# Attention layer and linear recurrence on one core: the recurrence laid out with key channels on partitions, in groups of 3, 3, 3, 3, 2, 2 batches instead of 4, 4, 4, 4

## Chip, cores and metric

One core of a Trainium2 chip runs the whole program. The metric is its device time in microseconds (us), lower is better. All data is float32.

## What is computed

The input has 16 batches of 112 rows of 512 channels and, per batch, a context of 375 rows. Two layers follow each other. The first is cross-attention with 16 heads of 32 channels and an MLP of inner width 2048. The second mixes each token with the one before it, runs a recurrence over time per head (32 heads of 16 key channels i and 16 value channels j), normalises its output per head, gates it, and ends with a squared-ReLU feed-forward part. Of the context, rows 0 and 1 and the rows 2 to 17 serve the second layer as the tokens before the first and as the start state.

```
attn = softmax(q @ k.T / sqrt(32) + mask) @ v            # layer 1, then c_proj, residual
y    = gelu(layernorm(h) @ fc_w + fc_b) @ proj_w         # MLP, residual
xm_j = xa + sx * (maa_stack_j + xxx_j)     j = 0..4      # token mixes: k, w, v, r, g
w    = exp(-exp(time_decay + tanh(xw @ td_w1) @ td_w2))
r, k, v, g = xr @ Wr.T, xk @ Wk.T, xv @ Wv.T, silu(xg @ Wg.T)
def step(s, (r, k, v, w)):                               # per head: s is 16 x 16, over 112 tokens
    a   = k[:, None] * v[None, :]
    out = sum_i r_i * (u_i * a_ij + s_ij)
    s   = a + w[:, None] * s
og   = groupnorm(out) * gn_w + gn_b;   x1 = x + (og * g) @ Wo.T
x1 + sigmoid(xr2 @ Wfr.T) * (relu(xk2 @ Wfk.T)**2 @ Wfv.T)
```

## The kernel before

The order is written out by hand, engine by engine, with semaphores. Batches go in groups of GB = 4, so the width of a group in tokens is T = 448. Products with a group's width hold 128 channels on the output's partitions and 448 tokens as columns.

The program of PE goes through groups g = 0 to 4. For g < 4 it does the *attention* of group g (`step`, 4 steps per batch, 16 in all), then the *MLP* of g (`mlp`). For g > 0 it does *post* of group p = g - 1 (Wo, layer norm, feed-forward, `post`), and for g < 4 the *token mix* of g (`pre`: low-rank products, decays, and the products for k, v, r and the gate). The recurrence of group p runs on DVE beside the attention and the MLP of g = p + 1. For the last group nothing is left to run beside it.

An attention step on PE is: the scores of the next step (`scores`, L304: four products onto one strip of rows each), the weighing of the values of the last step (`weigh`, L324: products onto 32 output partitions), and between four rounds of transposes (`turn`, L312, each waiting for ACT's exponents) the key and value projections of the next batch (L270). DVE takes the scores from PSUM, adds the mask and takes the row maximum (`masked`, L1020); ACT does the exponent and moves the transposed probabilities.

The recurrence (`scan_unit`) has one partition per batch and head (4 x 32 = 128). k, r and the decays w leave the token mix with channels on partitions, so POOL stores them to `rkw_scratch` and v to `v_scratch` in DRAM, and they are read back in the other layout. For each key channel i of 16, DVE makes r*u*k (L1067), k times v over all 16 value channels (L1069, 1792 columns with the start state at token 0, L1072), the sum of the bonus (L1075), two scans over time of 896 columns each (L1079, with the decays that ACT repeats for 8 value channels, L843), the product with r (L1083), and adds it to the output (L1091). These are UNITS = 5 sub-steps, UNITS_A_STEP = 3 of which stand in each attention step; the rest follows beside the MLP. In the last group the sum over i is done on PE with an identity product instead (`sum_channels`, L527). `group_norm` (L1100 to L1128) works in this layout; then SP writes `y_scratch` and reads it back with channels on partitions for `gate` (L1149, L1152).

The weights of the second half stream through a ring of SLOTS = 2 pieces of 1 MB each (`piece`, SP), 16 pieces per full group; a piece is loaded when the one two before it is used up. SP's queue is strict: the load of the start states, the wait for `y_norm` and the trip of y stand between ring pieces.

Of the kernel before, what the change touches and what calls it, by code (L numbers as in the profile page):

```python
# [5 lines left out]
F32 = mybir.dt.float32  # L6
# [11 lines left out]
GB = 4  # L18
NG = B // GB
# [4 lines left out]
JH = 8  # L24
# [13 lines left out]
ORDER = [1, 0, 2, 3, 4]  # L38

STORED = {1: 1, 2: 3, 3: 0}  # L40

W_MLP, W_POST, W_PRE = list(range(0, 8)), list(range(12, 16)), list(range(8, 12))


UNITS = 5
UNITS_A_STEP = 3
IN_STEPS = GB * HQ * UNITS_A_STEP

BLOCK = 2


def pieces_of(g):
    return [*(W_MLP if g < NG else []), *(W_POST if g > 0 else []), *(W_PRE if g < NG else [])]


PIECES = [p for g in range(NG + 1) for p in pieces_of(g)]
PIECE0 = [sum(len(pieces_of(k)) for k in range(g)) for g in range(NG + 1)]


# [30 lines left out]
def build(nc, x, ctxT, ctx, mask, shiftcols, cols, wq, wk, wv, wc, cproj_b, proj_b, stream,  # L90
          maa_w1, maa_w2, td_w1, td_w2, u, out):

    rkw_d = nc.dram_tensor("rkw_scratch", (B * RH, RS, 3, LQ), F32, kind="Internal").ap()
    v_d = nc.dram_tensor("v_scratch", (B * RH, RS * LQ), F32, kind="Internal").ap()
    y_d = nc.dram_tensor("y_scratch", (B * RH, RS * LQ), F32, kind="Internal").ap()

    ctxm = ExitStack()
    with ctxm:
# [6 lines left out]
        ident = sb("ident", [P, P])  # L105
        colt = sb("colt", [P, NCOL])
# [10 lines left out]
        ucol = sb("ucol", [P, RS])  # L117
# [14 lines left out]
        rden = sb("rden", [LQ, H])  # L132
        onT = sb("onT", [P, E, LQ])
# [9 lines left out]
        SX = sb("SX", [P, E * GB, LQ])  # L143
# [3 lines left out]

        VB = sb("VB", [P, RS, LQ])
        YB = sb("YB", [P, RS, LQ])
        rkw = sb("rkw", [P, 2, BLOCK, 3, LQ])  # L150
        s0 = sb("s0", [P, RS, RS])
        bon = sb("bon", [P, 2, LQ])
        gst = sb("gst", [P, 3, LQ])


        YT = SX[:, :, :].rearrange("p (e b) t -> p e (b t)", e=E)
        xnT = C[0]
        x_t = [HT[0:LQ, :, :].rearrange("p e t -> p (e t)")[:, k * D:(k + 1) * D] for k in range(2)]
        rdx = HT[0:LQ, :, :].rearrange("p e t -> p (e t)")[:, 2 * D:3 * D]
# [4 lines left out]
        XAs = XA[:, :, :, 1:LQ + 1]  # L164
        XAc = XA[:, :, :, :].rearrange("p e b t -> p (e b) t")
        wrep = XA[:, :, :, :].rearrange("p e b t -> p (e b t)")[:, 0:2 * JH * LQ].rearrange(
# [14 lines left out]
        def colb(name, n):  # L181
            k = COLS.index(name) * E
            return colt[:, k:k + E].unsqueeze(2).to_broadcast([P, E, n])
# [1164 lines left out]
```

## Time and profile before

| | us |
|---|---|
| median of 3 runs | 2032.33 |
| lowest and highest | 2018.66, 2036.81 |
| the profiled execution | 2021.98 |
| its span, first to last instruction | 2020.2 |
| PE busy in it | 1784.4 (88%) |
| DVE busy | 1176.1 (58%) |
| ACT busy | 637.1 (32%) |
| POOL busy | 223.3 (11%) |
| mean granted clock of TensorE | 0.92 |

An fp32 product appears as two matmul records; durations of neighbours overlap, so the pace is read from start to start. The granted clock has two levels, 1.00 (2.4 GHz) and 0.50 (1.2 GHz), and a mean says how much of a stretch ran at each. Idle PE is the length of a stretch less PE's busy time. "C<-..." names the tile written and the tiles read.

### The profile page before, as it was taken

To read this page: it belongs to the slowest core of one execution; us is meant where nothing else is said; L and a number is where in the kernel's file an instruction comes from. 1 tells how busy PE (TensorE), PEld (TensorE's weight loads), DVE (VectorE), ACT (ScalarE), POOL (GpSimd) and SP (SyncE) were. 2 spreads that over 40 slices of the span, in tenths; PEclk is the share of its full clock that TensorE was granted. 3 is DMA by queue.
4 is the path that set the end of the run, shared out by engine and by line. 5 is a ranking of instruction groups with operands and counts; after the bars stand their busy time and mean duration, and the time that the engine had idled before them with its cause. 6 is when DMAs were issued, how large, how long until landed. Compare 5 with 4: busy or idle time off the path is not lost.

```text
span 2020.2 us, 18127 instructions
## 1 busy us (share of the span) xinstructions
PE 1784.4 (88%) x6760; PEld 883.8 (44%) x6760; DVE 1176.1 (58%) x1649; ACT 637.1 (32%) x1480; POOL 223.3 (11%) x317
## 2 busy tenths in 40 slices
PE   6999998999999979999999979989779889856447
PEld 3555443445554433455554433445434334422223
DVE  1233002339988853449988654279988633299951
ACT  2566211136652112246641131256621131101011
POOL 1010000122210010122110010221200101100000
PEclk9999998799999989899999988999979987967868
DMA  7000021151102122341102321430012312400011
GB/s 234 26 26 21 22 83 63 62 160 33 40 27 77 63 99 81 96 125 40 53 14 71 105 76 60 128 97 32 14 34 84 103 47 85 146 25 21 7 57 39
DMA packets 73608, 135.15 MB, mean 67 GB/s; under 512 B 16241, under 2 KB 26993, under 8 KB 73521
## 3 DMA queue, kind: packets, MB, share of 16 engines
q1 hardware_dynamic: 59808, 101.05, 15.6%
q0 software_dynamic: 10496, 29.34, 4.7%
q10 hardware_dynamic: 3216, 3.60, 0.6%
q8 instruction: 55, 0.90, 0.2%
q14 instruction: 33, 0.26, 0.0%
HBM read 111.95 MB, written 22.02 MB: 66 GB/s over the span
## 4 chain that ended last, share of the span: by engine, by line
PE 68%; DVE 19%; issue 5%; DMA 3%; ACT 2%; ACTq 1%; POOL 1%; SPq 0%; DVEq 0%; POOLq 0%
PE bank L270 48%; PE bank L433 10%; DVE C L1079 5%; PE bank L497 3%; DVE sm L1020 3%; DVE C L1069 2%; PE bank L312 2%; DMA ring<-in_stream 2%; DVE YB L1091 1%; PE bank L304 1%; DVE C L1083 1%; DMA s<-in_ctx 1%; PE bank L324 1%; ACT XA L809 1%; PE bank L511 1%
## 5 line engine op out<-in xcount | busy, mean ns | idle before, releaser
L270 PE MATMUL bank<-C,ring 128*128 128x448 f32 x640 | 265.2, 577 | 17.9 <-DVE C L1131 17.9
L1079 DVE TENSOR_TENSOR_SCAN C<-XA,C 128x896 f32<-128x896 f32 x112 | 222.6, 2022 | 27.5 <-ACT XA L843 27.5
L433 PE MATMUL bank<-ring,HT 128*112 128x512 f32 x512 | 222.3, 592 | 0.0
L1020 DVE CUSTOM_DVE_ANT_0 sm<-bank,maskb 112x375 f32<-112x375 f32 x256 | 124.0, 541 | 166.5 <-PE bank L304 166.5
L270 PE MATMUL bank<-ctx_t,Wk 128*128 128x375 f32 x512 | 194.3, 504 | 13.4 <-DMA Wk<-in_wk 11.0
L270 PE MATMUL bank<-SX,ring 128*128 128x448 f32 x512 | 196.8, 543 | 7.8 <-ACT SX L809 7.8
L270 PEld LDWEIGHTS bank<-C,ring 128*128 128x128 f32 x640 | 128.5, 203 | 153.5 <-issue 149.6
L270 PE MATMUL bank<-Wv,ctx_t 128*125 128x512 f32 x384 | 182.3, 600 | 0.4 <-ACT C L809 0.4
L270 PE MATMUL bank<-ring,C 128*112 128x512 f32 x256 | 129.5, 662 | 56.1 <-issue 43.6
L312 PEld LDWEIGHTS bank<-ident,sm 112*125 112x125 f32 x768 | 123.5, 192 | 122.5 <-ACT sm L824 59.1
L830 ACT ACTIVATE probT<-bank 125x336 f32<-125x336 f32 x256 | 114.0, 445 | 145.8 <-PE bank L312 143.4
L824 ACT ACTIVATE sm<-sm,nm 112x375 f32<-112x375 f32 x256 | 153.5, 600 | 17.6 <-DVE nm L1020 17.3
L312 PE MATMUL bank<-ident,sm 112*125 112x112 f32 x768 | 128.3, 276 | 27.8 <-ACT probT L830 27.8
L433 PEld LDWEIGHTS bank<-ring,HT 128*112 128x112 f32 x512 | 90.6, 177 | 127.2 <-issue 127.2
L1232 DVE SCALAR_TENSOR_TENSOR C<-bank,colt,SX 128x448 f32<-128x448 f32 x80 | 53.6, 682 | 154.4 <-PE bank L497 152.7
L270 PEld LDWEIGHTS bank<-SX,ring 128*128 128x128 f32 x512 | 97.6, 191 | 104.6 <-issue 95.9
L891 ACT ACTIVATE HT<-bank,colt 128x448 f32<-128x448 f32 x64 | 40.5, 633 | 305.5 <-PE bank L270 305.5
L270 PEld LDWEIGHTS bank<-ctx_t,Wk 128*128 128x128 f32 x512 | 90.1, 195 | 62.0 <-issue 27.2
L1083 DVE TENSOR_TENSOR C<-C,rkw 128x1792 f32<-128x1792 f32 x56 | 113.3, 2023 | 1.8
L1069 DVE TENSOR_TENSOR C<-VB,rkw 128x1776 f32<-128x1776 f32 x56 | 112.0, 2001 | 0.1
L270 PEld LDWEIGHTS bank<-ring,C 128*112 128x112 f32 x256 | 49.8, 198 | 131.3 <-issue 119.9
L843 ACT ACTIVATE XA<-rkw 128x896 f32<-128x896 f32 x64 | 59.8, 949 | 131.4 <-DVE C L1083 68.1
(132 smaller groups left out, 2056.4 us busy)
## 6 DMA issues: line engine op xcount, KB each, us to landing
ring<-in_stream SPq DMA_DIRECT2D x64, 1024.0 KB, 5.5
ctx_t<-in_ctxT SPq DMA_DIRECT2D x16, 750.0 KB, 5.0
rkw_scratch<-HT POOLq DMA_DIRECT2D x48, 224.0 KB, 2.7
rkw<-rkw_scratch POOLq DMA_DIRECT2D x32, 224.0 KB, 3.1
HT<-in_x SPq DMA_DIRECT2D x16, 224.0 KB, 5.3
X<-in_x SPq DMA_DIRECT2D x16, 224.0 KB, 6.1
v_scratch<-HT POOLq DMA_DIRECT2D x16, 224.0 KB, 2.6
VB<-v_scratch SPq DMA_DIRECT2D x4, 896.0 KB, 7.1
```

The costliest lines, as they stand in the source:

```text
L270: last_ = nc.tensor.matmul(out_ap, pairs[k][0], pairs[k][1], start=(k == 0), stop=(k == len(pairs) - 1))
L312: last_ = nc.tensor.transpose(bank[k][0:KW, c * LQ:(c + 1) * LQ], sm[0:LQ, slot, c * KW:(c + 1) * KW], ident[0:LQ, 0:LQ])
L433: last_ = nc.tensor.matmul(bank[SC[b]][0:LQ, :], HT[:, c, b * LQ:(b + 1) * LQ], w[:, c, :], start=(m == 0 and c == 0), stop=(m == 3 and c ...
L497: closed(nc.tensor.matmul(bank[k][:, 0:T], w[:, e * P:(e + 1) * P], a, start=True, stop=True), ("LR", g, j, e), k)
L824: nc.scalar.activation(sm[0:LQ, slot, :], sm[0:LQ, slot, :], ACT.Exp, bias=nm[:, slot:slot + 1], scale=-1.0, accum_out=den[:, n % 2, e * H ...
L830: nc.scalar.activation(probT[:, r, :], tile(name)[0:KW, 0:KC * LQ], ACT.Copy).then_inc(freed(name), 1)
L843: nc.scalar.activation(wrep[:, i % 2, :].rearrange("p (j t) -> p j t", j=JH), rkw[:, (i // BLOCK) % 2, i % BLOCK, 2, :].unsqueeze(1).to_br ...
L1020: nc.vector.tensor_tensor_reduce(out=sm[0:LQ, slot, :], in0=tile(name)[0:LQ, 0:LK], in1=maskb[:, n % 2, :], scale=-SCALE, scalar=3.0e38, o ...
L1069: own.step(nc.vector.tensor_tensor(S[:, :, 1:LQ], VB[:, :, 0:LQ - 1], kk[:, 0:LQ - 1].unsqueeze(1).to_broadcast([P, RS, LQ - 1]), ALU.mult))
L1079: own.step(nc.vector.tensor_tensor_scan(out=part, data0=wrep[:, i % 2, :], data1=part, initial=0.0, op0=ALU.mult, op1=ALU.add))
L1083: prod = nc.vector.tensor_tensor(S[:, :, :], S[:, :, :], r.unsqueeze(1).to_broadcast([P, RS, LQ]), ALU.mult)
L1232: nc.vector.scalar_tensor_tensor(out=dst[:, e, :], in0=tile(name)[:, 0:T], scalar=col(f"maa_{ORDER[j]}", e), in1=SX[:, GB * e:GB * (e + 1) ...
```

## The change

Groups. The 16 batches go in six groups of 3, 3, 3, 3, 2 and 2, so widths are 336 and 224.

Layout. The recurrence now has the 128 key channels of eight heads on the partitions. k, r and the decays stay where the token mix leaves them (tiles KS, R and W). Only v goes through DRAM: POOL stores it, one token late, and reads it back per unit with each head's row repeated on its 16 key channels (`load_unit`). A unit is one of 4 channel blocks e and 4 value channels j of each head: 16 units a group, with columns j, batch, token (4 x 336 or 4 x 224). DVE does four sub-units on each (`sub_unit`): product with k, in place, and start state (L1221, L1224); a scan of half the columns (L1230), a scan of the other half; product with r (L1236). Three buffers take turns. There is no add on DVE: the sum over the key channels of a head is four products on PE per unit, each with a selecting matrix onto 32 output partitions (`sum_unit`, L418), for every group. DVE adds the finished block to the bonus (`y_add`, L1259). The decays are repeated by ACT once per block e instead of once per i, straight out of the exponent.

Bonus and norm. The bonus is r*u*k on DVE and one product per block with a matrix of heads (L632) in the token mix. Mean and variance per head are products with an averaging matrix (`means` L430, `variances` L437) between those of the MLP; ACT squares and takes Ln and Exp for the deviation; DVE applies norm and gate in four blocks. Nothing goes through DRAM and back.

Order. `Plan` holds at which attention step or at which of the 32 chunks of the MLP each sum stands, and how many of the 64 sub-units stand in the attention (44 of 12 steps for 3 after 3, 36 of 8 for 2 after 3, 48 of 8 for 2 after 2). Wo follows the MLP, or comes before its last quarter in the last group. The scores and exponents of the next group's first step now stand before the gate product. The token mix makes v first, then k, r and g. SP loads the start states after the ring's pieces as before, in group order, and has no trip of y. Weighed values share the bank of the transposes (6), and bank 7 collects the recurrence.

```diff
-GB = 4
-NG = B // GB
+SIZES = [3, 3, 3, 3, 2, 2]
...
-ORDER = [1, 0, 2, 3, 4]
+ORDER = [1, 2, 0, 3, 4]
...
+NJ = 4
+UNITS = E * (RS // NJ)
+STAGES = 4
+SUBS = UNITS * STAGES
+BUFS = 3
...
+IN_STEPS = {(3, 3): 44, (3, 2): 36, (2, 2): 48}
...
+            def sum_unit(p, unit):
+                e, q = divmod(unit, UNITS // E)
+                if q == 0:
+                    opened(Y_BANK)
+                pe.wait_ge(z_ready, p * UNITS + unit + 1)
+                n = width(p)
+                for s in range(NJ):
+                    last_ = nc.tensor.matmul(bank[Y_BANK][HD * s:HD * (s + 1), 0:n], sel[:, q, :],
+                                             unit_tile(p, unit)[:, s * n:(s + 1) * n],
+                                             start=(q == 0), stop=(q == UNITS // E - 1))
...
-            def sum_channels(p):
-                for k in SC:
-                    opened(k)
...
+            def load_unit(p, unit):
...
+                rows = v_d[p][e, q, :, :, :].rearrange("h s t -> h (s t)")
+                pool.dma_start(unit_tile(p, unit), rows.unsqueeze(1).to_broadcast([8, RS, NJ * width(p)])
+                               ).then_inc(s_in[unit % BUFS], 16)
...
-                elif stage == 4 and not last:
-                    own.settle()
-                    nc.vector.tensor_tensor(YB[:, :, :], YB[:, :, :], S[:, :, :], ALU.add).then_inc(scan_step, 1)
...
+                    own.step(nc.vector.tensor_tensor(
+                        S[:, :, :, 1:LQ], S[:, :, :, 1:LQ],
+                        KS[:, e, 0:n, 1:LQ].unsqueeze(1).to_broadcast([P, NJ, n, LQ - 1]), ALU.mult))
...
+                elif stage in (1, 2):
+                    own.settle()
+                    dve.wait_ge(wrep_ready, p * E + e + 1)
+                    part = flat[:, (stage - 1) * 2 * nt:stage * 2 * nt]
...
+                else:
+                    own.settle()
+                    js = flat.rearrange("p (j t) -> p j t", j=NJ)
+                    nc.vector.tensor_tensor(js, js, R[:, e, 0:nt].unsqueeze(1).to_broadcast([P, NJ, nt]), ALU.mult
+                                            ).then_inc(z_ready, 1)
```

DVE in the recurrence of the last group, before: one key channel for four batches.

```order
L1067 SCALAR_TENSOR_TENSOR bon<-rkw,ucol 128x112
L1069 TENSOR_TENSOR HT<-VB,rkw 128x16x111
L1072 COPY HT<-s 128x16
L1075 TENSOR_TENSOR bon<-bon 128x112
L1079 SCALAR_TENSOR_TENSOR HT<-XA,HT 128x896 x2
L1083 TENSOR_TENSOR HT<-HT,rkw 128x1792
```

The same place now: two units for two batches (the scans are printed as SCALAR_TENSOR_TENSOR in both).

```order
L1221 TENSOR_TENSOR C<-C,KS 128x8x111
L1224 COPY C<-s 128x8
L1230 SCALAR_TENSOR_TENSOR C<-XA,C 128x448 x2
L1236 TENSOR_TENSOR C<-C,R 128x896
L1221 TENSOR_TENSOR SA<-SA,KS 128x8x111
L1224 COPY SA<-s 128x8
L1230 SCALAR_TENSOR_TENSOR SA<-XA,SA 128x448 x2
L1236 TENSOR_TENSOR SA<-SA,R 128x896
```

The two small operations for the bonus have left; every remaining one is half as wide.

PE in the MLP of a group, before: products and nothing between them, then (not printed) the wait for Wo.

```order
L270 MATMUL bank<-SX,ring 128x448 x16
L433 MATMUL bank<-ring,HT 112x512 x16
L270 MATMUL bank<-SX,ring 128x448 x16
L433 MATMUL bank<-ring,HT 112x512 x16
L270 MATMUL bank<-SX,ring 128x448 x16
```

PE now, at the end of the MLP of group 4 (two batches, with the recurrence of three beside it).

```order
L418 MATMUL bank<-C,sel 32x336 x4
L334 MATMUL bank<-SX,ring 128x224 x12
L550 MATMUL bank<-ring,HT 112x512 x2
L418 MATMUL bank<-SA,sel 32x336 x4
L550 MATMUL bank<-ring,HT 112x512 x4
L430 MATMUL bank<-BV,mean 128x336 x4
L550 MATMUL bank<-ring,HT 112x512 x2
L437 MATMUL bank<-R,mean 128x336 x4
L334 MATMUL bank<-ring,C 112x512 x12
```

Two sums, the means and the variances (L418, L430, L437) have come between the MLP's products; the variances are its last and Wo (L334, ring,C) follows at once.

PE in an attention step now, with one sum (L418) between the second and third round of transposes, where there was none.

```order
L376 MATMUL bank<-ident,sm 125x112 x3
L418 MATMUL bank<-C,sel 32x336 x4
L334 MATMUL bank<-Wv,ctx_t 125x512 x2
L376 MATMUL bank<-ident,sm 125x112 x3
L334 MATMUL bank<-Wv,ctx_t 125x512 x2
```

The sum waits for DVE's product with r, and the transposes behind it wait with it.

## Rows read from the trace of the kernel before

**Rows 1.** Windows: length, busy PE, PEld, DVE, ACT, POOL, TensorE clock, DMA share, GB/s.
```profile
58.00:1762.00 1704.00, 1594.21 (x6378) 799.90 (x6376) 991.92 (x1468) 594.40 (x1406) 202.10 (x269) 0.94 0.21 67
58.00:209.00 151.00, 147.84 (x998) 86.84 (x996) 46.46 (x163) 90.88 (x252) 11.12 (x20) 1.00 0.08 25
331.00:437.00 106.00, 95.47 (x217) 43.83 (x216) 36.16 (x63) 22.18 (x44) 18.40 (x28) 0.79 0.26 81
437.00:595.00 158.00, 149.80 (x998) 86.64 (x996) 149.74 (x241) 101.22 (x263) 32.05 (x30) 1.00 0.18 55
722.00:795.00 73.00, 62.42 (x161) 28.00 (x162) 32.10 (x61) 18.64 (x45) 8.54 (x19) 0.91 0.13 43
1323.00:1478.00 155.00, 134.82 (x918) 80.05 (x917) 143.71 (x224) 91.06 (x239) 24.63 (x21) 0.92 0.12 39
1762.00:1912.00 150.00, 85.57 (x128) 35.69 (x128) 138.97 (x117) 16.64 (x18) 8.64 (x12) 0.72 0.09 28
1912.00:1940.00 28.00, 0.08 (x1) 0.11 (x1) 17.78 (x14) 0.39 (x1) 0.00 (x0) 0.59 0.20 66
```

**Rows 2.** Timeline of PE in an attention step of the second group.
```profile
459.48 0.90 PE L304 MATMUL bank<-KT,qT 32*112 32x375 f32 x8
460.31 0.78 PE L324 MATMUL bank<-probT,V 125*32 125x112 f32 x24
461.02 1.53 PE L270 MATMUL bank<-ctx_t,Wk 128*128 128x375 f32 x4
```

**Rows 3.** Timeline of PE from the MLP of the second group to its post.
```profile
665.43 12.19 PE L270 MATMUL bank<-SX,ring 128*128 128x448 f32 x32
677.46 13.90 PE L433 MATMUL bank<-ring,HT 128*112 128x512 f32 x32
691.19 12.19 PE L270 MATMUL bank<-SX,ring 128*128 128x448 f32 x32
...
722.42 15.54 PE L270 MATMUL bank<-ring,C 128*112 128x512 f32 x32 [5.31 <-issue]
...
740.93 1.06 PE L292 MATMUL bank<-ident,xn 112*128 112x112 f32 x8 [2.20 <-DVE xn L1002]
746.71 13.65 PE L270 MATMUL bank<-C,ring 128*128 128x448 f32 x32 [4.72 <-DVE C L1131]
...
765.71 5.36 PE L270 MATMUL bank<-ring,C 128*112 128x512 f32 x8 [2.40 <-DMA ring<-in_stream]
```

**Rows 4.** Timeline of DVE at the start of the last recurrence.
```profile
1770.64 0.33 DVE L1067 SCALAR_TENSOR_TENSOR bon<-rkw,ucol 128x112 f32<-128x112 f32 x1 [30.05 <-DMA s<-in_ctx]
1770.89 2.00 DVE L1069 TENSOR_TENSOR C<-VB,rkw 128x1776 f32<-128x1776 f32 x1
...
1773.21 3.93 DVE L1079 TENSOR_TENSOR_SCAN C<-XA,C 128x896 f32<-128x896 f32 x2
1777.18 2.02 DVE L1083 TENSOR_TENSOR C<-C,rkw 128x1792 f32<-128x1792 f32 x1
1779.31 0.33 DVE L1067 SCALAR_TENSOR_TENSOR bon<-rkw,ucol 128x112 f32<-128x112 f32 x1
```

**Rows 5.** Timeline of DVE after the last norm.
```profile
1935.98 1.78 DVE L1149 TENSOR_SCALAR C<-C,colt 128x448 f32<-128x448 f32 x4 [9.47 <-DMA C<-y_scratch]
```

**Rows 6.** Timeline of PE in the last post.
```profile
1939.92 16.07 PE L270 MATMUL bank<-ring,C 128*112 128x512 f32 x32 [28.18 <-issue]
...
1964.23 14.17 PE L270 MATMUL bank<-C,ring 128*128 128x448 f32 x32 [4.08 <-DVE C L1131]
1983.68 6.07 PE L270 MATMUL bank<-ring,C 128*112 128x512 f32 x8 [5.28 <-issue]
```

**Rows 7.** DMA issues of the page: count, size, median us to landing.
```profile
ring<-in_stream SPq DMA_DIRECT2D x64, 1024.0 KB, 5.5
rkw<-rkw_scratch POOLq DMA_DIRECT2D x32, 224.0 KB, 3.1
VB<-v_scratch SPq DMA_DIRECT2D x4, 896.0 KB, 7.1
```

More of the change, by code:

```diff
@@ L17 @@
 INNER = 4 * D
-GB = 4
-NG = B // GB
+SIZES = [3, 3, 3, 3, 2, 2]
+NG = len(SIZES)
+START = [sum(SIZES[:g]) for g in range(NG + 1)]
+GROUP = [(g, b) for g in range(NG) for b in range(SIZES[g])]
+GB = max(SIZES)
 T = GB * LQ
@@ L60 @@
+PIECES = [(g, piece) for g in range(NG + 1) for piece in pieces_of(g)]
+PIECE0 = [sum(len(pieces_of(k)) for k in range(g)) for g in range(NG + 2)]
 class Chain:
@@ L105, in build @@
         ident = sb("ident", [P, P])
+        sel = sb("sel", [P, 4, HD])
+        heads = sb("heads", [P, P])
+        mean = sb("mean", [P, P])
         colt = sb("colt", [P, NCOL])
@@ L368, in step @@
                 turn(n, e, 1)
+                if g > 0:
+                    for unit in range(UNITS):
+                        if PLAN[g].sum_step.get(unit) == b * HQ + e:
+                            sum_unit(g - 1, unit)
                 if e == 0 and b > 0:
@@ L404, in channels_out, with chunk @@
                             pe.wait_ge(blocks[0], blocks[1] + c + 1)
-                        last_ = product(bank[k][:, 0:T], pairs, c, c + 1)
+                        last_ = product(bank[k][:, 0:n], pairs, c, c + 1)
                     closed(last_, names[e], k)
+                    if between is not None:
+                        between(e)
+            def chunk(g, at):
+                if g == 0:
+                    return
+                for unit in range(UNITS):
+                    if PLAN[g].sum_chunk.get(unit) == at:
+                        sum_unit(g - 1, unit)
+                if at == PLAN[g].means:
+                    means(g - 1, shared)
+                if at == PLAN[g].variances:
+                    variances(g - 1, shared)
             def mlp(g):
-                n = g * GB + GB - 1
+                n, last, nt = START[g + 1] - 1, g + 1 == NG, width(g)
                 weigh(n, E - 1)
-                if g + 1 < NG:
-                    for b in range(GB):
-                        evacuated(pe, ("TX", (g + 1) * GB + b))
+                if not last:
+                    for b in range(SIZES[g + 1]):
+                        evacuated(pe, ("TX", START[g + 1] + b))
                     query(g + 1, 0)
@@ L606, in _ @@
             load_mask(0)
-            load_xt(2)
-            load_xt(3)
+            for b in range(2, SIZES[0]):
+                load_xt(b)
             load_ctx(1)
@@ new lines, in mix_block, with shift_and_mix @@
+            def mix_block(g, sx, dst, name, e):
+                return nc.vector.scalar_tensor_tensor(
+                    out=by_batch(dst[:, e, 0:width(g)], g), in0=by_batch(sx[:, e, 0:width(g)], g),
+                    scalar=col(name, e), in1=XA[:, e, 0:SIZES[g], 1:LQ + 1], op0=ALU.mult, op1=ALU.add)
+            def shift_and_mix(which, g, sx, dst, name, done):
+                n = SIZES[g]
+                own.step(nc.vector.tensor_copy(XA[:, :, 0:n, 0], shc[:, which, :, START[g]:START[g + 1]]))
@@ L1216, in pre @@
             def pre(g):
-                if g == 0:
-                    for b in range(GB):
-                        pre_stats(g, b)
-                    pre_rows(g)
+                nt = width(g)
                 for j in range(5):
@@ L1255, in _ @@
             nc.vector.tensor_tensor(cb[:, :], tile(("VC",))[0:LQ, :], cb[:, :], ALU.add).then_inc(freed(("VC",)), 1)
-            def units(p, lo, hi):
-                for unit in range(lo, hi):
-                    scan_unit(p, unit)
+            masked(0, 0)
             for g in range(NG + 1):
```

952 lines of the change are left out of this document (525 added, 427 removed).

## Prediction, made before the changed kernel was run

> **What bounds the kernel now.** I read the windows first. Before the last part, from 58 to 1762 us, PE works 1594 of 1704 us and sits idle for 110 [rows 1]. Clock is lost too: 0.94 on average, 0.79 in the first token mix. DVE comes close to PE only in attention: 149.7 of 158 us in the second group, where PE has 149.8. The attention of the first group, with no recurrence beside it, takes 151 us, so DVE costs little there. After 1762 us it is the other way round: the recurrence of the last four batches runs alone for 150 us with PE waiting for DVE, its norm takes 28 us with PE empty, and four batches of post take 80. This tail is 258 us, 13% of the span. So the change is a trade: a shorter tail, which DVE sets, against more work and more joints in the 1762 us that PE sets.
>
> I then read PE's timeline for paces. Matmul records stand two to an fp32 product. In the MLP, 32 records of 448 columns take 12.03 us (0.376 each) and 32 of 512 take 13.73 (0.429) [rows 3]: 0.00083 us per column and almost nothing fixed. 336 columns then take 0.283 us, 224 take 0.190. Products that fill only a strip of the array overlap: 8 records of the scores in 0.83 us, 24 of 112 columns onto 32 outputs in 0.71 [rows 2].
>
> **The tail, -120 us.** Its time today is 2020.2 - 1762.
> - Start. DVE waits for the start states until 1770.6 [rows 4]. The new SP order again puts those loads behind the ring pieces, so 8 of the 9 us stay.
> - Recurrence. A pass costs 8.67 us from start to start: product 2.00, two scans 3.93, product 2.02, small ones 0.7 [rows 4]. The new unit of the last group is 888 and 896 elements per product and 448 per scan: 1.0 + 0.2 + 1.97 + 1.01 + 0.1 for the settles = 4.3 us, 16 times = 69. (A four-batch i needs 8.67; two batches need half of it, and the order shows no more work than that.)
> - Norm. Today 28 us, of which 9.5 is the way through DRAM [rows 5]. The new chain is last sum, add, mean product, subtraction, square, product, Ln, Exp, two DVE operations: ten short links near 1 us. I take 11; it can't be below 6 (the same operations back to back at half of their present widths) nor above the 28.
> - Post. Now 16 us for Wo, 8.4 to the first ffn product, 14.2 of it, 5.3 for the ring, 30 for the last products, 6.4 to the end [rows 6]. With two batches the products halve, the waits stay: 8 + 8 + 7 + 5 + 15 + 7 = 50.
> Sum 8 + 69 + 11 + 50 = 138 instead of 258.
>
> **More matmul work before the tail, +119 us.** PE is the bound there, so it counts nearly in full.
> - Sums over key channels. 16 units of four products onto 32 partitions each, for five groups (those of the sixth lie in the tail, under DVE). The trace has no such product; the nearest is the weighing of the values, also four strips of 32 outputs: 0.71 / 24 / 112 per column and record gives 0.72 us per unit of three batches and 0.48 of two [rows 2]. The scores' pace gives 0.74. 64 x 0.72 + 16 x 0.48 = 54, less 3 beside the last batch, where PE idles anyway: 51. The upper end is no overlap at all: 2.26 and 1.52 us a unit, 169 in all. The strips are laid out as the weighing's are, so I take 51. The identity products of today (85.6 us in the tail [rows 1]) lay under DVE and give nothing back.
> - Bonus, mean and variance: sets of eight records, 3 x 4 groups x 8 x 0.283 = 27, and 4 x 8 x 0.19 = 6. Sum 33.
> - Narrow products: each group has 392 records whose width is the group's, and there are two groups more. Columns stay the same, so only the fixed part counts: 0.005 to 0.02 us each, 4 to 16 us. I take 8.
> - Post of batches 13 and 14, formerly in the tail: half of its products at full clock: Wo 32 x 0.429, the first ffn product 32 x 0.376, the other two 64 x 0.429, 53 us; so 27.
>
> **Idle PE before the tail, 110 to 142 us.** Today, by stage: attention 38 (3.2, 8.2 and 20.2 in the groups shown), MLP with its end 27, post 31 (10.6 in the group shown), token mix 14 [rows 1].
> - Attention: about 44. Beside the recurrence DVE needs 46.46 / 16 = 2.9 us a step (first group), and 3 sub-steps of 2.17 give the 9.4 us that the second group shows (149.74 / 16). A three-batch unit is 6.2 us by its elements [rows 4], so 3.67 sub-units make 5.7 + 2.9 = 8.6 us a step against 9.0 + 0.7 on PE: less tight than today. The scores and exponents of the next group now stand before the gate product, which hides most of the 5 us that each start costs. But in 2-after-3 DVE has 4.5 sub-units a step (9.9 us against 9.7), and in the very last batch, with no keys left to project, six of 1.07 us: DVE needs 9.3 us a step and PE has 4. So 3 in the first group, 3 x 3, 5, and 27 in the last (20 today).
> - MLP: about 36. Today Wo starts 5.3 us late [rows 3], since DVE finishes late and SP holds the Wo piece behind the DRAM trip. That gap goes. In its place ACT swaps tables for Ln and Exp between two Gelus (2 us a group), and in the 2-after-3 group the mean product stands in chunk 30 and the variance in chunk 32 of 32, so the norm's chain, about 9 us, ends after the MLP.
> - Post: 46. The wait after Wo (layer norm, transposes, mixing) and the wait for the last ring piece are 2.2 + 4.7 and 2.4 us per group [rows 3], and neither depends on width: now five times instead of three, though one of them lies under the MLP of the last group.
> - Token mix: 16.
>
> **Clock: 0.** A gap of 5 us before Wo, followed by half clock, falls away each time; two more token mixes and two more posts bring one each. Bounds -40 to +20 from the 0.79 and the 0.94 [rows 1].
>
> **Sum.** -120 + 119 + 32 = +31. The profiled execution took 2022 us (span 2020.2), so 2053. The median of the three timed runs lies 10 us above it, the highest at 2037; I add nothing for that and let the range take it. A measurement of this kernel can tell about 1% (20 us) from no change.
>
> **DMA.** The loads of units are 672 KB (448 for two batches), 96 in all, and ring pieces grow from 64 to 96. A load of that size lands in 4.4 us at the ring's pace (from 224 KB in 3.1 to 1024 KB in 5.5) and 5.8 at the pace of the one large read back from scratch (896 KB in 7.1) [rows 7]. Three buffers cover that: in the tail, load 4.4 + unit 4.3 + sum 1.2 + issue 1 = 10.9 against 3 x 4.3 = 12.9. A ring piece is used for 9.1 to 10.3 us in groups of three and 6.1 to 6.9 in groups of two, both above 5.5. So I price DMA at nothing.
>
> **Rivals.**
> - A, not slower. The planned placing of sums and sub-units keeps idle PE at 110 or below: no queue runs late because each sum is placed a step behind its product, and the 2-after-3 norm is hidden. Then -120 + 119 - 5 gives 2016. For it: the 5.3 us gap goes three times and DVE has less work per batch (16 x 6.2 / 3 = 33 us instead of 16 x (8.67 + 2.02 for the add) / 4 = 43). Against it: post's waits are chains of dependent operations that the change doesn't shorten. It decides from an idle sum below about 120 us before the tail.
> - B, faster through the clock. The stretches of narrow-row products (low rank, decay) in which the clock falls to half are shorter per group, and if it stays up, up to 40 of the time lost before the tail come back: 2013 from mine, 1976 with A.
> - C, late unit loads. If the bytes came at half the pace of the large read, loads would take 9.8 and 7.1 us. Then the tail's cycle is 13.6 against 12.9 (+4 us), each step of the 2-after-2 group waits some 2 us (+16), and the others 8: 2081. The Trainium skill, "DMA: Bandwidth & Descriptors", section "Why a DMA increments its semaphore by 16 and not by 1", says that a DMA uses as many engines, up to 16, as divide the slowest dimension of both patterns. The source here has eight heads outermost, so by it these loads use eight engines. No row of this trace shows such a load; the sum above goes without it.
> - D, the sums don't overlap: 2053 + 115 = 2168.
>
> **Chances.** Mine 0.45, 2034 to 2072; A 0.27; B 0.08; C 0.14; D 0.06. Bounds of the unknowns within mine: idle +10 to +55, narrow products -4 to +8, norm -5 to +8. Faster by over 1% (below 2012): a third of A and all of B, 0.17. Slower by over 1% (above 2053): C, D and half of mine, 0.43. Between: the rest, 0.40. Range 1998 to 2110, which leaves out D and the lower part of B with A.
>
> **What would show it.** In the new profile: the tail near 138 us with units 4.3 us apart; sum products at 0.7 us a unit inside attention; no gap before Wo except in the fifth group; the waits after Wo and for the ring as long as now, in more groups; PE busy near 1810 us in all. I am wrong if idle PE before the tail is not above 120 us, if a sum costs 2 us, or if DVE waits for DMA in the 2-after-2 group.

## The result, and the profile after

The changed kernel takes 2152.76 us (median of four runs, 2149.15 to 2153.97), against 2025.49 for the kernel before in the same session: a ratio of 1.063, interval 1.055 to 1.070. The forecast was 2053, so it missed by 100 us, and the time lies outside its range.

The windows of the changed kernel, from attention start to attention start, one row a group, and the tail last. Columns as in [rows 1].

```profile
58.00:351.00 293.00, 278.33 (x1233) 159.71 (x1230) 71.08 (x197) 103.37 (x268) 15.57 (x29) 0.93 0.19 55
351.00:713.00 362.00, 335.89 (x1493) 182.82 (x1492) 197.59 (x324) 125.22 (x308) 43.21 (x54) 0.95 0.34 92
713.00:1075.00 362.00, 335.63 (x1498) 182.68 (x1500) 198.46 (x325) 126.02 (x308) 41.83 (x54) 0.95 0.33 92
1075.00:1437.00 362.00, 336.32 (x1506) 184.33 (x1507) 199.17 (x329) 126.76 (x308) 42.75 (x53) 0.95 0.34 93
1437.00:1735.00 298.00, 248.96 (x1191) 154.34 (x1193) 172.31 (x269) 92.14 (x232) 34.22 (x45) 0.91 0.41 104
1735.00:2004.00 269.00, 222.11 (x1072) 144.37 (x1072) 134.68 (x258) 81.36 (x205) 25.51 (x38) 0.84 0.33 96
2004.00:2152.00 148.00, 57.18 (x232) 26.85 (x232) 87.19 (x122) 17.66 (x38) 11.18 (x20) 0.63 0.23 69
```

The six groups add up to 1946 us with PE busy for 1757, so it is idle for 189. Before, it was busy for 1594 of 1704 and idle for 110 [rows 1]. The three parts of the forecast, against the profiled span:

| part | before | after | difference | predicted |
|---|---|---|---|---|
| tail | 258 | 148 | -110 | -120 |
| PE busy ahead of the tail | 1594 | 1757 | +163 | +119 |
| PE idle ahead of the tail | 110 | 189 | +79 | +32 |
| span | 2020.2 | 2152.2 | +132 | +31 |

So the tail did roughly what was expected. It fell 10 us short, and the rest of what is missing lies in front of it: 44 us of matmul time and 47 us of waiting.

The issues by size in the changed kernel's profile (count, size, median us to landing) answer to [rows 7]. Below them, the waits: us in total, times, the longest.

```profile
ring<-in_stream SPq DMA_DIRECT2D x96, 1024.0 KB, 5.5
SA<-v_scratch POOLq DMA_DIRECT2D x44, 672.0 KB, 8.2
C<-v_scratch POOLq DMA_DIRECT2D x20, 672.0 KB, 8.3
ctx_t<-in_ctxT SPq DMA_DIRECT2D x16, 750.0 KB, 7.5
SA<-v_scratch POOLq DMA_DIRECT2D x22, 448.0 KB, 5.7
C<-v_scratch POOLq DMA_DIRECT2D x10, 448.0 KB, 6.5
```
```profile
DVE SA L1221 <- DMA s<-in_ctx: 63.5, 6, 11.7
```

The unit loads land in 8.2 us, not in the 4.4 to 5.8 of the forecast, and DVE waits for the start states six times: at the head of five attentions and of the tail. One such place, the fourth group's attention, is worth reading on three engines. First SP's queue, with the issue of each load:

```profile
1074.96 0.37 SPq L726 DMA_DIRECT2D ring<-in_stream  x1
1075.49 1.56 SPq L747 DMA_DIRECT2D s<-in_ctx  x3
1077.10 1.20 SPq L721 DMA_DIRECT2D X<-in_x  x1
1078.35 0.60 SPq L715 DMA_DIRECT2D mrow<-in_mask  x1
1078.99 0.60 SPq L704 DMA_DIRECT2D ctx_t<-in_ctxT  x1
```

Then DVE:

```profile
1077.19 0.54 DVE L1174 CUSTOM_DVE_ANT_0 sm<-bank,maskb 112x375 f32<-112x375 f32 x1
1077.66 0.08 DVE L1174 DVE_READ_ACCUMULATOR2_ANT nm<- 112x1 f32 x1
1089.21 1.55 DVE L1221 TENSOR_TENSOR SA<-SA,KS 128x1332 f32<-128x1332 f32 x1 [11.46 <-DMA s<-in_ctx]
```

And PE:

```profile
1086.99 1.89 PE L334 MATMUL bank<-Wv,ctx_t 128*125 128x512 f32 x4
```
```profile
1097.93 0.94 PE L376 MATMUL bank<-ident,sm 112*125 112x112 f32 x3 [9.05 <-ACT probT L946]
1098.67 3.64 PE L334 MATMUL bank<-Wv,ctx_t 128*125 128x512 f32 x4
```

The three loads of 32 KB are issued at 1075.5, right behind a ring piece of 1 MB, and with rows and context behind them they land some 12 us later. DVE has masked the first four scores by 1077.7 and then stands before its first product. The next scores are done but their masking is queued behind that product, so ACT gets no exponents and PE nothing to transpose: PE's row names ACT, the cause is two engines further up. After the 9 us gap the same four records of 512 columns take 3.64 us instead of 1.89, and the windows show the clock of each and, second to last, the share of the DMA engines:

```profile
1097.90:1103.00 5.10, 5.07 (x14) 2.82 (x17) 5.03 (x5) 2.16 (x7) 3.16 (x2) 0.50 0.00 0
1080.00:1088.00 8.00, 6.86 (x55) 4.43 (x56) 0.00 (x0) 3.15 (x10) 0.00 (x0) 1.00 1.09 167
```

After the gap PE runs at half of its 2.4 GHz. And while DVE waits, the DMA engines are full (1.09 of their number, at 167 GB/s), so I read it that the small loads wait for the large ones; the first experiment tests that.

The second place is the group of two after three. DVE's first products of a unit, with what they waited for:

```profile
1527.19 1.55 DVE L1221 TENSOR_TENSOR SA<-SA,KS 128x1332 f32<-128x1332 f32 x1 [1.44 <-DMA SA<-v_scratch]
1560.03 1.55 DVE L1221 TENSOR_TENSOR SA<-SA,KS 128x1332 f32<-128x1332 f32 x1 [10.66 <-DMA SA<-v_scratch]
1586.69 1.54 DVE L1221 TENSOR_TENSOR C<-C,KS 128x1332 f32<-128x1332 f32 x1 [1.02 <-DMA C<-v_scratch]
1597.56 1.55 DVE L1221 TENSOR_TENSOR SA<-SA,KS 128x1332 f32<-128x1332 f32 x1 [4.38 <-DMA SA<-v_scratch]
```

and PE's in the same MLP:

```profile
1566.49 1.35 PE L418 MATMUL bank<-SA,sel 128*32 128x336 f32 x8 [7.49 <-DVE SA L1236]
...
1574.84 0.77 PE L418 MATMUL bank<-C,sel 128*32 128x336 f32 x8
...
1626.51 3.97 PE L334 MATMUL bank<-ring,C 128*112 128x512 f32 x5 [7.00 <-DVE C L1279]
```

DVE waits 17.5 us for unit loads here. The sum of a late unit stops PE for 7.5 us in the middle of the MLP. The norm comes 7 us late for Wo; that gap is not the loads' doing, for it is 7.00 us as well in the kernel in which they are quick (f1, below), and the forecast had this chain at about 9. The second sum row is what such a sum costs by itself: 0.77 us.

The tail on DVE answers to [rows 4]:

```profile
2013.30 1.08 DVE L1221 TENSOR_TENSOR SA<-SA,KS 128x888 f32<-128x888 f32 x1 [9.05 <-DMA s<-in_ctx]
...
2017.76 1.08 DVE L1221 TENSOR_TENSOR SA<-SA,KS 128x888 f32<-128x888 f32 x1
```

Nine us for the states, then units 4.45 us apart.

### The profile page after: what moved, and what is told of

Read it like the earlier page. It is cut to its first block, busy times and chain, and to the rows that moved or that the text cites. A ratio compares the mean times of both kernels' runs of the same rounds, so it can differ in the third digit from the quotient of the medians.

```text
span 2152.2 us, 22035 instructions
## 1 busy us (share of the span) xinstructions
PE 1855.3 (86%) x8328; PEld 1057.1 (49%) x8328; DVE 1067.5 (50%) x1836; ACT 685.3 (32%) x1689; POOL 228.1 (11%) x333
## 2 busy tenths in 40 slices
DMA packets 104728, 194.76 MB, mean 90 GB/s; under 512 B 28688, under 2 KB 37424, under 8 KB 104624
## 3 DMA queue, kind: packets, MB, share of 16 engines
q0 software_dynamic: 26624, 66.16, 12.4%
## 4 chain that ended last, share of the span: by engine, by line
PE 73%; DVE 9%; DMA 7%; issue 5%; ACT 4%; ACTq 1%; SPq 0%; POOL 0%; DVEq 0%; POOLq 0%
PE bank L334 50%; PE bank L550 8%; DMA s<-in_ctx 3%; PE bank L376 3%; DVE SA L1230 3%; PE bank L623 2%; DMA ring<-in_stream 2%; PE bank L368 2%; PE bank L418 2%; DMA SA<-v_scratch 2%; PE bank L387 2%; PE bank L646 1%; DVE C L1230 1%; ACT XA L925 1%; PE bank L356 1%
## 5 line engine op out<-in xcount | busy, mean ns | idle before, releaser
L334 PE MATMUL bank<-C,ring 128*128 128x336 f32 (+1 forms) x960 | 275.1, 448 | 26.2 <-DVE C L1284 17.2
L334 PEld LDWEIGHTS bank<-C,ring 128*128 128x128 f32 x960 | 195.5, 207 | 105.1 <-issue 40.1
L334 PE MATMUL bank<-SX,ring 128*128 128x336 f32 (+1 forms) x768 | 211.6, 434 | 14.2 <-ACT SX L925 8.5
L334 PE MATMUL bank<-ctx_t,Wk 128*128 128x375 f32 x512 | 194.4, 504 | 14.8 <-DMA Wk<-in_wk 11.3
L334 PE MATMUL bank<-Wv,ctx_t 128*125 128x512 f32 x384 | 191.4, 624 | 0.4 <-ACT C L925 0.4
L334 PEld LDWEIGHTS bank<-SX,ring 128*128 128x128 f32 x768 | 152.4, 201 | 75.4 <-issue 20.1
L1230 DVE TENSOR_TENSOR_SCAN SA<-XA,SA 128x672 f32<-128x672 f32 (+1 forms) x132 | 186.6, 1414 | 3.6
L376 PE MATMUL bank<-ident,sm 112*125 112x112 f32 x768 | 130.3, 279 | 49.8 <-ACT probT L946 47.8
L334 PE MATMUL bank<-ring,C 128*112 128x512 f32 x256 | 131.8, 670 | 36.0 <-issue 21.8
L1039 ACT ACTIVATE HT<-bank,colt 128x336 f32<-128x336 f32 (+1 forms) x96 | 48.8, 510 | 346.3 <-PE bank L334 346.3
L1221 DVE TENSOR_TENSOR SA<-SA,KS 128x1332 f32<-128x1332 f32 (+1 forms) x66 | 92.5, 1401 | 90.9 <-DMA s<-in_ctx 63.5
L1371 DVE SCALAR_TENSOR_TENSOR C<-bank,colt,SX 128x336 f32<-128x336 f32 (+1 forms) x120 | 58.7, 526 | 158.0 <-PE bank L623 158.0
L334 PEld LDWEIGHTS bank<-ctx_t,Wk 128*128 128x128 f32 x512 | 90.5, 196 | 64.0 <-issue 28.0
L418 PE MATMUL bank<-SA,sel 128*32 128x336 f32 (+1 forms) x528 | 53.5, 482 | 76.1 <-DVE SA L1236 75.1
L334 PEld LDWEIGHTS bank<-ring,C 128*112 128x112 f32 x256 | 50.7, 201 | 110.0 <-issue 110.0
L334 PEld LDWEIGHTS bank<-Wv,ctx_t 128*125 128x125 f32 x384 | 67.1, 194 | 69.9 <-issue 69.9
```

The lines of the kernel that those rows point to most:

```text
L334: last_ = nc.tensor.matmul(out_ap, pairs[k][0], pairs[k][1], start=(k == 0), stop=(k == len(pairs) - 1))
L376: last_ = nc.tensor.transpose(bank[k][0:KW, c * LQ:(c + 1) * LQ], sm[0:LQ, slot, c * KW:(c + 1) * KW], ident[0:LQ, 0:LQ])
L418: last_ = nc.tensor.matmul(bank[Y_BANK][HD * s:HD * (s + 1), 0:n], sel[:, q, :], unit_tile(p, unit)[:, s * n:(s + 1) * n], start=(q == 0), ...
L1039: nc.scalar.activation(HT[:, e, 0:width(g)], tile(name)[:, 0:width(g)], ACT.Gelu_apprx_tanh, bias=colt[:, FCB + 4 * m + e:FCB + 4 * m + e + 1]
L1221: own.step(nc.vector.tensor_tensor(S[:, :, :, 1:LQ], S[:, :, :, 1:LQ], KS[:, e, 0:n, 1:LQ].unsqueeze(1).to_broadcast([P, NJ, n, LQ - 1]), ...
L1230: own.step(nc.vector.tensor_tensor_scan(out=part, data0=wrep[:, e % 2, 0:2 * n, :].rearrange("p n t -> p (n t)"), data1=part, initial=0.0, ...
```

## The experiments

Times are medians of the timed runs; ratios are to the kernel before of the same session, with the 95% interval. The kernel before had 2025, 2025, 2022, 2021 and 2030 in the five sessions.

### The start states early (e1, e2)

```
-                if g > 0:                     # head of SP's turn for a group
-                    for b in range(SIZES[p]): sp.dma_start(s0[...], ctx[START[p] + b, ...])
                 for at in range(PIECE0[g] + SLOTS, ...):
+                    if g < NG and at == PIECE0[g + 1]:      # ahead of the next group's first two pieces
+                        if g > 0: ready(sp, ("Y", g - 1, E - 1))
+                        for b in range(SIZES[g]): sp.dma_start(s0[...], ctx[START[g] + b, ...])
                     piece(at)
```

> The changed kernel with one edit: SP issues the loads of the start states ahead of the last two ring pieces of a token mix, not behind them. Theory 1 (late states): in the changed kernel every attention from the second group on opens with DVE waiting 11.5 us for these loads (63.5 us in six waits), the masked scores queue behind that wait, and PE then waits 9 us for exponents. Then DVE's wait for the states falls below 5 us in all, PE's wait for the exponents from 48 to below 15 us, the start of the tail from 14 to about 3 us, and the time by 45 to 60 us. Rival: the loads of the first units, the decays or the exponents end almost as late, so the wait only changes its name: the time falls by 0 to 15 us.

Measured 2112.45 us, ratio 1.042 (1.037 to 1.048): 40 us off the changed kernel. DVE's wait for the states is gone from the profile altogether. PE's wait for exponents fell from 47.8 us to 27.2, not to below 15. The gain is a little under the 45 us of the theory's lower end, and far above the 15 of the rival; but the rival is right in part. DVE now waits for the next input rows, whose load SP issues behind the ring piece and the context:

```profile
1071.08 0.69 DVE L1152 BATCH_NORM_STATS2 bst_ln<-HT 112x6 f32<-112x512 f32 x1 [7.23 <-DMA HT<-in_x]
```

There are four such waits of 6.9 to 8.0 us, one in each of the four middle attentions; in the changed kernel this wait occurs only once, at the very start of the program. So 29 of the 63.5 us that DVE waited came back under another name, where PE's longest wait for exponents is 4.0 us and no longer 9.3.

> The kernel before with the same move of its start states. Theory 1 says that the late states are a flaw of both kernels' SP queue, but that before lost less by it, since its scan waited for keys and values on their way through DRAM as well: 0 to 15 us less, most of it in the tail. Rival: it loses as much as the changed kernel, 8 us in each of four places: 30 us less.

Measured 2021.59, ratio 1.002 (0.998 to 1.006): nothing that can be told from no change. The same order of SP's queue costs the kernel before nothing measurable and the changed one 40 us. The waits of DVE (us in total, times, longest) show why. In the kernel before, and with its states early:

```profile
DVE bon L1067 <- DMA s<-in_ctx: 43.5, 4, 30.0
```
```profile
DVE bon L1067 <- DMA VB<-v_scratch: 37.8, 4, 27.3
```

Here the wait does change its name: the values on their way through DRAM arrive almost as late as the states did.

### Unit loads of sixteen rows (e3), and a control (g2)

```
-    v_scratch{g}: (E, RS // NJ, 8, NJ, SIZES[g] * LQ)
+    v_scratch{g}: (E, RS // NJ, 8, 2, NJ, SIZES[g] * LQ)       # each head's values stored twice
-    rows = v_d[p][e, q, :, :, :].rearrange("h s t -> h (s t)")
-    pool.dma_start(unit_tile(p, unit), rows.unsqueeze(1).to_broadcast([8, RS, NJ * width(p)]))
+    rows = v_d[p][e, q, :, :, :, :].rearrange("h c s t -> (h c) (s t)")
+    pool.dma_start(unit_tile(p, unit), rows.unsqueeze(1).to_broadcast([16, RS // 2, NJ * width(p)]))
```

> The changed kernel, with the values stored twice in DRAM so that a unit's load has sixteen rows outermost, not eight. If loads of eight rows are slow because they are spread over eight engines, a 672 KB load lands in about 5 us rather than 8.2, and if that costs time (ring pieces late in groups of two, units late) the time falls by 10 to 30 us. Rival 1: landing falls, time stays within 5 us, since three buffers cover it. Rival 2: landing stays at 8 us, and the time rises by a few us through the added stores.

Measured 2095.27 us, ratio 1.035 (1.031 to 1.040): 57 us less, twice what was expected at most, in spite of the added stores. The landings:

```profile
SA<-v_scratch POOLq DMA_DIRECT2D x44, 672.0 KB, 5.3
ctx_t<-in_ctxT SPq DMA_DIRECT2D x16, 750.0 KB, 4.8
```

The unit loads land as they were priced in the forecast, and other loads gain with them: the context from 7.5 to 4.8 us, and DVE's wait for the states from 63.5 to 44.0. By the attention starts in PE's timelines the 57 us lie in the group of two after three (301 to 279 us, -22), the three middle groups (-11 together), the last group up to its token mix (211 to 200, -11), and the rest at both ends.

> Both edits, but the loads read eight rows again, out of the values stored twice: a control. If the rows are the cause, the landing is back at 8.2 us and the time at that of the early states alone, 2105 to 2120. If the layout or spacing in DRAM was the cause, the landing stays near 5.3 us and the time near 2055.

Measured 2102.10, ratio 1.040 (1.033 to 1.047), and the 672 KB loads land in 8.2 and 8.8 us. The time is 3 us below the expected 2105 to 2120 and within 10 of the kernel with the early states alone. So neither the second copy nor the spacing in DRAM made the loads quick.

### Both (f1)

> The changed kernel with both edits: start states early, and unit loads of sixteen rows. Theory 2 (two separate waits): the early states gave 8 us in each group of three after the first and nothing in the group of two after three, where the recurrence was late anyway; the quick loads gave 22 us just there and 11 in the last group. They add up or better: 85 to 105 us off the changed kernel's 2152, so 2047 to 2067. Rival: they remove the same waiting of PE for DVE and overlap by half: 2070 to 2085.

Measured 2055.20 us, ratio 1.016 (1.012 to 1.020): 98 us off the changed kernel, within 1 us the sum of 40 and 57. The two waits are separate, as the theory had it. Its windows, one row a group and the tail:

```profile
58.00:344.00 286.00, 271.60 (x1227) 155.95 (x1225) 70.57 (x195) 102.90 (x268) 18.21 (x33) 0.95 0.20 59
344.00:695.00 351.00, 333.81 (x1492) 182.07 (x1492) 195.93 (x323) 125.17 (x308) 43.25 (x58) 0.96 0.33 97
695.00:1048.00 353.00, 335.79 (x1504) 182.64 (x1502) 197.40 (x326) 126.92 (x309) 42.72 (x59) 0.96 0.33 96
1048.00:1396.00 348.00, 331.48 (x1488) 181.84 (x1488) 195.05 (x320) 123.69 (x303) 43.48 (x56) 0.96 0.34 97
1396.00:1671.00 275.00, 249.08 (x1214) 154.18 (x1211) 174.17 (x284) 96.04 (x238) 35.20 (x51) 0.95 0.40 116
1671.00:1916.00 245.00, 215.34 (x1061) 141.70 (x1059) 132.36 (x254) 79.60 (x202) 26.28 (x42) 0.85 0.35 107
1916.00:2053.00 137.00, 55.44 (x232) 26.19 (x232) 86.81 (x121) 17.27 (x38) 10.06 (x20) 0.65 0.24 74
```

PE is busy for 1737 of 1858 us ahead of the tail and idle for 121, and the tail is 138. Of the matmul time that was missing from the forecast, 20 us went with the waits although no product was removed. The value projections of the attentions (L334, Wv) account for 7.6 of them (191.4 us before the two edits, 183.8 now) and the MLP's first products in the groups of two (L334, SX,ring, 224 columns) for 7.0 (61.9, now 54.9); both stand behind waits that went, and after such a wait PE ran at half clock.

### What in the load is slow (g1, h1)

> Both edits, with the values stored four times, so that a unit's load has 32 rows outermost. If the number of rows sets how many DMA engines share a load and sixteen is all there are, a 672 KB load lands in 5.3 us as with 16 rows, and the time is that of both edits (2055) or up to 10 us more through 16 more stores a... (each 5 to 7 us long, outside the path). Rival: more and smaller pieces land faster still, 4 us or less.

Measured 2067.85 us (2054.14 to 2080.86), ratio 1.023 (1.014 to 1.032). The 672 KB loads land in 4.2 and 4.1 us: faster than the theory said, close to its rival. The time is not below that of both edits, and lies 13 us above by the medians, though its runs spread over 27 us and the quickest lies within those of both edits; the stores are now 64, at a median of 10.3 us. So eight rows take 8.2 us, sixteen 5.3, thirty-two 4.2. But along that series each address is read by sixteen, eight and four partitions, so a second reason was open.

```
-    pool.dma_start(unit_tile(p, unit), rows.unsqueeze(1).to_broadcast([8, RS, NJ * width(p)]))
+    pool.dma_start(unit_tile(p, unit), rows.unsqueeze(0).to_broadcast([RS, 8, NJ * width(p)]))
```

> The changed kernel with the states early, values stored once, and a unit's load read in another order: the 16 copies outermost and the 8 heads within, the same addresses as often as before. The heads then stand on other partitions, so the recurrence takes values of other heads; amounts and waits are the same. It tells two reasons apart for which a load of eight rows took 8.2 us, one of sixteen 5.3 and one of 32 4.2. Theory rows (the slowest dimension of the source shares a load among the DMA engines): sixteen outermost, so 5.3 us and a time near 2055. Theory addresses (each address was read 16, 8 and 4 times in these, and repeated reads of one place are what is slow): 8.2 us or more and a time near 2105.

Measured 2058.59 us, ratio 1.012 (1.008 to 1.016). The landings of this kernel:

```profile
SA<-v_scratch POOLq DMA_DIRECT2D x44, 672.0 KB, 5.4
```

The same bytes from the same addresses, each as often as in the changed kernel, land in 5.4 us instead of 8.2 to 8.5 when sixteen stands outermost instead of eight. The reads of one place are cleared; the order of the dimensions decides. The queue that issues these loads tells how (the line gives packets, MB, and the time of its packets as a share of the span on 16 engines). In e1, with eight outermost:

```profile
q0 software_dynamic: 26624, 66.16, 13.1%
```

and here, with sixteen:

```profile
q0 software_dynamic: 16384, 66.11, 12.9%
```

The same MB occupy the engines for nearly the same time in all (13.1% of 16 x 2110.4 us and 12.9% of 16 x 2059.9), but a load is over in 5.4 us rather than 8.4. So with eight rows fewer engines should work on a load at once, and the traces show it. These are stretches in which one load of 672 KB runs alone: 5.9 us of e1 (367.8 to 373.7), 3.4 us of this kernel (380.7 to 384.1) and 2.45 us of g1, with 32 rows (380.5 to 382.95).

```profile
q0 software_dynamic: 136, 0.69, 48.3%
```
```profile
q0 software_dynamic: 144, 0.69, 90.2%
```
```profile
q0 software_dynamic: 144, 0.69, 80.9%
```

48.3% of 16 engines are 7.7 at work on average, 90.2% are 14.4. That agrees with the rule that the Trainium skill gives in "DMA: Bandwidth & Descriptors", section "Why a DMA increments its semaphore by 16 and not by 1", and that the prediction named beside rival C: eight heads outermost use eight engines. The further step from 5.3 to 4.2 us with 32 rows is of another kind. There 12.9 engines are at work, no more than with sixteen, but a packet occupies one for 0.22 us (80.9% of 16 x 2.45 us over 144 packets) instead of 0.34 in the two other stretches. Why is open: each address is read by four partitions there, and by sixteen in e1 and here, so for this step the number of reads is not cleared.

### The price of the sums (e4, g3)

```
-    matmul(bank[Y_BANK][HD * s:HD * (s + 1), 0:n],  sel[:, q, :], unit_tile(p, unit)[:, s * n:(s + 1) * n], ...)
+    matmul(bank[Y_BANK][HD * s:HD * (s + 1), 0:16], sel[:, q, :], unit_tile(p, unit)[:, s * n:s * n + 16], ...)
```

> The changed kernel with the sum products cut to 16 columns each: the sums over key channels are left out but for those columns, every wait stays. If PE sets the time nearly everywhere before the tail, the 62 us of sum records go: 50 to 62 us less. If DVE sets the groups of two, the part of theirs comes back as waiting: 30 to 45 us less.

Measured 2125.68, ratio 1.050 (1.044 to 1.055): 27 us less, below both statements but near the second. The cut took less away than the expectation reckoned with: the products of 16 columns still have 20 of the 61 us of sum records ahead of the tail, so 41 went.

> Both edits, with the sum products cut to 16 columns, so that the sums are left out but for those. With unit loads on time PE should bound more of the time before the tail than in the changed kernel, where the same cut gave 27 us. Theory: 40 to 55 us less than both edits (2000 to 2015), near the 51 of the prediction. Rival: PE waits for DVE beside attention instead, whatever the loads do: 20 to 30 us less again (2025 to 2035).

Measured 2023.30, ratio 1.000 (0.997 to 1.003): 32 us less than both edits, nearer to the rival. In this pair, too, some 40 us of records went. By the attention starts, the three middle groups of three (f1 346 to 1397, here 350 to 1371) are 10 us shorter each, where the records of the sums fell from 12.4 us to 4.1; the group of two after three is 4 shorter, from 12.9 to 4.1; the last stays at 195 up to its token mix, from 10.2 to 3.7. A matmul costs its full time where PE sets the pace, half of it or nothing where PE waits for DVE anyway.

### More and less of the recurrence beside attention (f2, f3)

> Both edits, and more of the recurrence placed inside the attention of the groups of two (44 and 54 of 64 sub-units, before 36 and 48). If those groups still wait for a recurrence that ends after the MLP has room for it, 5 to 15 us less than both edits alone. If DVE is full beside attention (77 of 86 us now), the attention gets longer by 8 sub-units of 1.55 us and the time rises by 5 to 15 us.

Measured 2067.29, ratio 1.021 (1.018 to 1.025): 12 us more than both edits. The attention of the group of two after three (up to the first product of its MLP) became 14 us longer and its MLP 8 shorter; the last attention became 8 longer with nothing given back. DVE is full beside attention, as the second statement has it.

> Both edits, and less of the recurrence inside the attention of the groups of two (28 and 40 of 64). If DVE is what bounds the attention of a group of two (PE 67 of 86 us in the last), it gets shorter by 10 us in each group and the MLP takes the work up: 5 to 15 us less than both edits alone. If the norm at the end of the recurrence is then late for Wo, 5 to 20 us more.

Measured 2061.50, ratio 1.018 (1.013 to 1.023): 6 us more by the medians, with runs that overlap those of both edits (2056 to 2067 against 2051 to 2061), so it is not less, and more is not shown. The attention of the last group became shorter by 3 us, not by 10, and what follows up to the token mix longer by 11; the group of two after three kept its attention and its MLP ran 5 longer. The 36 and 48 of the changed kernel were no worse than either of the other two settings, so the number of sub-units placed there is not what is lost.

### One more group (f5)

> Both edits, in groups of 3,3,2,2,2,2,2: two groups of three become three groups of two. Joints that do not depend on the width cost 25 us of idle PE a group by the windows (12 at the start of attention, 10 in post, 3 elsewhere), less 8 with the states early, and a group of two beside a group of two is bound by DVE in attention (19 us of idle PE in the last). Theory: 25 to 45 us more than both edits in groups of 3,3,3,3,2,2. Rival (the price of a joint is only in the last two groups, whose last attention has no next batch): 0 to 15 us more.

Measured 2089.88, ratio 1.032 (1.028 to 1.036): 35 us more for one group more. Its second group of three, and its three groups of two after two (length, then busy PE):

```profile
347.00:695.00 348.00, 331.28 (x1489) 181.83 (x1488) 194.91 (x321) 123.84 (x303) 43.14 (x56) 0.96 0.34 97
...
967.00:1212.00 245.00, 228.26 (x1177) 150.10 (x1176) 137.24 (x272) 91.05 (x231) 30.68 (x47) 0.95 0.39 115
1212.00:1455.00 243.00, 224.58 (x1177) 146.91 (x1176) 137.01 (x272) 90.83 (x231) 30.88 (x47) 0.96 0.38 117
1455.00:1696.00 241.00, 223.87 (x1182) 147.65 (x1181) 137.82 (x274) 91.00 (x232) 30.85 (x47) 0.97 0.39 118
```

Three groups of two after two take 245 + 243 + 241 = 729 us for six batches, two groups of three 2 x 348 = 696. PE is busy for 677 of the 729 and for 663 of the 696. So of the 33 us between them 14 are matmul time, the price of narrower products, and 19 are the idle joint, which is 17 us a group in either size.

## Why the prediction was wrong

**The step that failed.** "So I price DMA at nothing" was one line, and by the time it carried nearly the whole error: 98 of 100 us. It rested on two things. The landing was put at 4.4 to 5.8 us "at the ring's pace" and "at the pace of the one large read"; it is 8.2, since neither of the two rows has eight rows outermost (57 us in e3, and 54 from e1 to h1). And the start states were seen behind the ring pieces, but charged only in the tail, "8 of the 9 us stay", while for the attentions "the scores and exponents of the next group now stand before the gate product, which hides most of the 5 us that each start costs". The first scores are early, but DVE's queue closes behind them, and the next masks stand behind the wait for the states (e1: 40 us). So DMA at nothing was in truth 98 us, and with both mended the kernel takes 2055.2, where the forecast was 2053.

**That this agrees so well is partly luck.** Term by term, with f1, in which few of these waits are left (PE's wait for exponents is 17.3 us):

| term | predicted | changed kernel | f1 |
|---|---|---|---|
| tail | -120 | -110 | -121 |
| PE busy ahead of it | +119 | +163 | +143 |
| PE idle ahead of it | +32 | +79 | +11 |

In f1 the busy time is 24 us above the forecast and the idle time 21 below it; the two errors cancel.

- Tail, right. Start 9 us (8 predicted), recurrence 72 (69), from the last sum to Wo 14 (11), the rest 53 (50).
- Sums, size near, price wrong. A unit's sum takes 0.77 us, 0.72 was said, and the strips overlap (2.26 us was the price without overlap): rival D falls. The records ahead of the tail add up to 61 us where 51 was said; the units of two batches take 0.67 us, not 0.48. Taking two thirds of that out gives 27 to 32 us: "PE is the bound there, so it counts nearly in full" holds in the groups of three and not in the groups of two.
- Bonus, mean, variance: 38 us of records against 33.
- The remaining matmul time is 64 us (163 less 61 and 38) against 35 for "post of batches 13 and 14" and "narrow products". Some 20 of these 64 went with the waits in f1; most of that is clock lost after them, for which the forecast had "0". The rest, 9 us, I put down to an undersized width effect: the products of "C,ring" and "SX,ring" have the same columns in all as before, and their records take 482 us in f1 against 462 before, where 8 us was said. f5 shows the same in another place, 14 us more busy PE for six batches in twos than in threes.
- Idle PE, 142 forecast, 189 measured, 121 without the two waits. Post was right (45 us). Attention was put at 44 and took 73, the MLPs at 36 and took 45, token mix 16 and took 26 (stages by finer windows); the last holds two waits for a ring piece, 9 us, in the groups of two.
- "I am wrong if DVE waits for DMA in the 2-after-2 group" came true, up to 5.0 us at a time. It was worse in the group before.

**The rivals.** C, late unit loads, had the right mechanism and half the price: 28 us forecast, 57 measured, although it put the loads at 9.8 and 7.1 us and they take 8.2 and 5.7 to 6.5. It counted the tail, the last group and 8 us elsewhere. In the tail no unit load is waited for. It did not see that the group of two after three, in which 64 sub-units of full width stand beside two thirds of the other work, has the least room for a late load (-22 us in e3), nor that the slow loads hold up others. A would be near in f1 by its idle time (121 against its bound of 120), but not by its time. B, a clock that stays up, did not come: the mean granted clock is 0.92 before, 0.91 in the changed kernel and 0.92 in f1.

**What is left.** f1 is still 33 us above the kernel before in the profiled executions: -121 in the tail and +154 ahead of it. Cutting the sums gives 32 of that back (g3, which then equals the kernel before), and the third of their records that this cut leaves could give up to 16 more in proportion, an estimate. Bonus, mean and variance are 38 by their records, the post of two batches 27 by the forecast's rows, and two groups more 54 at f5's price of 27 (by the spans; by the medians it is 35, and then 70). With 32 for the sums these add up to 151, and with the higher figures to 183, so the list accounts for the 154 only roughly. The post of two batches and the two groups are reckoned, not shown: a way with groups of four, or the post term alone, was not tried. No version that was run beats the kernel before.

## What to carry to other kernels

Price a new transfer by a row with the same shape, above all the same outermost dimension, and if the trace has none, give it a bound that is wide, and look at what a miss costs where buffers are fewest. Follow small loads through their queue to the instruction that waits for them, and then ask what stands behind that instruction: loads of 32 KB that come 11 us late at the head of each group cost here 40 us in all, because the masking of scores was queued behind the wait, and the same lateness cost the other kernel nothing, because another load was as late. And a kernel cut into more groups pays for each twice, here with 14 us in narrower products and 19 in one more idle joint.

## What was not expected of the hardware

- A broadcast load of 672 KB takes 8.2 us with eight rows outermost, 5.3 with sixteen rows, 5.4 with sixteen copies outermost of the same eight rows, 4.2 with thirty-two rows.
- One load of 672 KB alone has 7.7 DMA engines at work on average with eight outermost (e1), 14.4 with sixteen (h1) and 12.9 with 32 (g1), where its packets are shorter instead, 0.22 us against 0.34.
- The load with eight outermost is cut into more packets: 26,624 against 16,384 on its queue for the same bytes, all of the difference below 512 B (28,688 against 18,448 in the whole kernel).
- Such loads slow others that run beside them: the context's 750 KB land in 7.5 us beside them and in 4.6 to 5.0 beside the quick ones.
- Three loads of 32 KB, issued 0.5 us behind a load of 1 MB and ahead of the 750 KB of the context, were there only some 12 us after their issue, with the DMA engines' share at 1.09 in between.
